# Rank terms of a channel attention on four row groups of the array, behind the value weights

## The reference

```
def _channel_attention(qm, km, vm, scale):
    qh, kh, vh = (heads of qm, km, vm as b, h, d, n)
    scores = jnp.einsum('bhdn,bhen->bhde', qh, kh) * scale
    attn = jax.nn.softmax(scores, axis=-1)
    out = jnp.einsum('bhde,bhen->bhdn', attn, vh)
...
att_global = _channel_attention(q * wqg + bqg, k * wkg + bkg, v * wvg + bvg, scale)
att_local = _channel_attention(q * wql + bql, k * wkl + bkl, v * wvl + bvl, scale)
xattn = 2.0 * (att_global + att_local) * wp + bp
x = x + tanh(g_xattn[0]) * xattn(_layernorm(x), ctx, ctx)
x = x + tanh(g_ffn[0]) * ffn(_layernorm(x))   # two linear layers, int8-like quantised, gelu
```

## Time and profile before

| | us |
|---|---|
| median of 3 runs | 369.76 (368.94 to 369.95) |
| the profiled execution, its own time | 368.73 |
| its span, first to last instruction | 366.9 |
| TensorE busy | 349.0 (95%) |
| VectorE busy | 330.2 (90%) |
| ScalarE busy | 285.2 (78%) |
| GpSimd busy | 119.8 (33%) |
| mean granted TensorE clock | 0.984 |

### The profile page before, as it was taken

One profiled execution on the slowest core, in us unless ns is written; L12 is line 12 of the kernel. 1 busy time (PEld: TensorE's weight loads), 2 busy tenths in 40 slices (PEclk: granted clock), 3 DMA queues, 4 the chain that ended last, 5 costly groups with the idle time before them and its releaser, 6 DMA issues.

```text
span 366.9 us, 6644 instructions
## 1 busy us (share of the span) xinstructions
PE 349.0 (95%) x2406; PEld 245.9 (67%) x2418; DVE 330.2 (90%) x630; ACT 285.2 (78%) x493; POOL 119.8 (33%) x178
## 2 busy tenths in 40 slices
PE   6979989999999888999999999999999999999995
PEld 4667767887886775554545455454548888888884
DVE  3698999999999978999999988987769999999996
ACT  1465879889886965879859988789799999999520
POOL 2644578778689790069000000421000000000000
PEclk9869999999999999999999999999999999999999
DMA  7999978565311463767748760000191999995225
GB/s 222 378 404 403 401 278 280 196 228 216 117 37 80 145 203 128 290 268 312 290 200 341 319 260 0 1 2 0 51 409 56 383 395 424 424 422 233 102 116 229
DMA packets 22963, 84.78 MB, mean 231 GB/s; under 512 B 2129, under 2 KB 11857, under 8 KB 14482
## 3 DMA queue, kind: packets, MB, share of 16 engines
q1 hardware_dynamic: 22272, 83.89, 59.2%
q10 hardware_dynamic: 658, 0.46, 0.4%
HBM read 54.99 MB, written 29.36 MB: 230 GB/s over the span
## 4 chain that ended last, share of the span: by engine, by line
PE 60%; DVE 19%; ACT 10%; issue 5%; DMA 3%; POOL 2%; SPq 1%; DVEq 0%; ACTq 0%; POOLq 0%
PE PS L1460 19%; PE PS L1415 17%; PE PS L1257 7%; DVE hmax L1042 7%; PE PS L1318 6%; ACT ring L703 5%; DMA X<-in_x 3%; PE PS L1299 3%; DVE hmax L832 2%; ACT ring L616 2%; PE PS L1266 2%; PE PS L1312 2%; DVE ring L1019 2%; PE PS L1289 1%; PE PS L1278 1%
## 5 line engine op out<-in xcount | busy, mean ns | idle before, releaser
L683 ACT ACTIVATE ring<-PS,bias,sc 128x512 f32<-128x512 f32 x128 | 97.1, 783 | 21.6 <-PE PS L1415 6.6
L1415 PE MATMUL PS<-mid,w1q 128*128 128x512 bf16 x500 | 110.7, 379 | 1.9 <-DVE mid L996 1.2
L1415 PEld LDWEIGHTS PS<-mid,w1q 128*128 128x128 bf16 x512 | 49.7, 98 | 59.9 <-DVE mid L996 0.7
L1042 DVE TENSOR_REDUCE hmax<-ring 128x1 f32<-128x2048 f32 x30 | 67.4, 2278 | 5.6 <-ACT ring L683 5.6
L703 ACT ACTIVATE ring<-ring,sc 128x2048 int16<-128x2048 f32 x29 | 55.6, 1987 | 0.0
L1460 PE MATMUL PS<-w2q,ring 128*128 128x256 f16 x336 | 39.0, 273 | 0.0
L1257 PE MATMUL PS<-ring 128*128 128x129 f32 x256 | 33.8, 296 | 2.0 <-DVE ring L741 1.5
L1460 PEld LDWEIGHTS PS<-w2q,ring 128*128 128x128 f16 x336 | 32.9, 98 | 4.0
L1257 PEld LDWEIGHTS PS<-ring 128*128 128x128 f32 x256 | 33.0, 212 | 3.1 <-issue 3.1
L1170 DVE SCALAR_TENSOR_TENSOR X<-PS,sc,X 128x512 f32<-128x512 f32 x48 | 35.0, 739 | 0.0
L1318 PEld LDWEIGHTS PS<-w2q,ring 128*128 128x128 f32 x256 | 29.2, 192 | 6.7 <-issue 6.7
(11 more groups left out here) (147 smaller groups left out, 586.8 us busy)
## 6 DMA issues: line engine op xcount, KB each, us to landing
spilled_hidden<-ring SPq DMA_DIRECT2D x20, 1024.0 KB, 3.9
ring<-spilled_hidden SPq DMA_DIRECT2D x20, 1024.0 KB, 9.1
ring<-in_ctxT SPq DMA_DIRECT2D x8, 1024.0 KB, 5.4
ring<-in_ctx SPq DMA_DIRECT2D x8, 896.0 KB, 8.4
X<-in_x SPq DMA_DIRECT2D x7, 1024.0 KB, 9.5
out<-X SPq DMA_DIRECT2D x7, 1024.0 KB, 9.6
ring<-in_w1T SPq DMA_DIRECT2D x4, 1024.0 KB, 13.4
ring<-in_w2T SPq DMA_DIRECT2D x8, 512.0 KB, 3.4
```

The costliest lines, as they stand in the source:

```text
L683: nc.scalar.activation(ring[:, s * CH + c, (h % CH) * N:(h % CH + 1) * N], PS[:, hidden_bank(s, h), :], ACT.Gelu, scale=SC1, bias=bias1[:, ...
L1042: V.tensor_reduce(hmax[:, bass.ds(CH * g + c, 1)], ring[:, s * CH + c, :], AX.X, ALU.max, apply_absolute_value=True).then_inc(hm_done, 1)
L1415: mm = nc.tensor.matmul(PS[:, hidden_bank(s, h), :], w1v[:, k, h * P:(h + 1) * P], xqT[:, s, k, :], start=(k == 0), stop=(k == NH - 1))
```

## The change

The rank terms become four products, one for each attention and each pair of heads, on the row groups 0 to 31, 32 to 63, 64 to 95 and 96 to 127, with 256 columns each, in banks 2, 3, 4 and 5 (the first half of each bank). `L_sb`, `Rh`, `rowc` and `psK` so have 128 partitions; `Rh`, `rowc` and `psK` have 256 columns. `sel` is wider and the key sums are two products of 256 columns. Since banks 2 and 3 are those of psT, the rank terms of batch b + 1 now wait for `m_done`, the value weights of batch b, which read psT. On VectorE the value weights go ahead of the constant row in passes 0 to 6. In pass 7 the warming products in bank 2 wait for the scores. The host lays out `blocks` and `turned` for the new places, `ones` moves to another buffer, and 64 more columns of `small` are used.

The diff, cut to its core (the layouts on the host and the widths of buffers are left out):

```
-        sel = cut(64)
+        sel = cut(P + 32)
...
-        Rh = mid[:, 0:512]
-        rowc = mid[:, 512:1024]
+        ones = w2f[:, 0:P]
+        Rh = mid[:, 0:2 * P]
+        rowc = mid[:, 512:512 + 2 * P]
...
-        psR = PS[:, 4:6, :].rearrange("p a (h e) -> p (a h) e", e=P)
-        psA = PS[0:64, 4, 0:P]
-        psK = PS[0:64, 5, :]
+        psR = PS[:, 2:6, 0:2 * P].rearrange("p q (h e) -> p q h e", e=P)
+        psA = PS[:, 4, 0:P]
+        psK = PS[:, 5, 0:2 * P]
...
-                nc.gpsimd.tensor_tensor(Rh[0:64, :], Rh[0:64, :], rowc[0:64, :], ALU.mult).then_inc(rh_done, 1)
+                nc.gpsimd.tensor_tensor(Rh, Rh, rowc, ALU.mult).then_inc(rh_done, 1)
...
-                nc.scalar.activation(L_sb[0:64, :], psA, ACT.Copy).then_inc(L_done, 1)
+                nc.scalar.activation(L_sb, psA, ACT.Copy).then_inc(L_done, 1)
...
                 elif b >= 0:
+                    value_weights(b)
                     constant_row(b)
                     if b == B - 2:
                         w1_scale()
-                    value_weights(b)
...
-                nc.tensor.matmul(psK, sel, ksum.rearrange("p h e -> p (h e)"), start=True, stop=True).then_inc(sk_done, 1)
+                for a in range(2):
+                    mm = nc.tensor.matmul(psK, sel[:, 32 - 32 * a:32 - 32 * a + P],
+                                          ksum[:, 2 * a:2 * a + 2].rearrange("p h e -> p (h e)"),
+                                          start=(a == 0), stop=(a == 1))
+                mm.then_inc(sk_done, 1)
...
                 pe.wait_ge(L_done, b + 1)
                 pe.wait_ge(rh_done, b + 1)
-                for g in range(2):
-                    mm = nc.tensor.matmul(PS[:, 4 + g, :], L_sb[32 * g:32 * g + 32, :], Rh[32 * g:32 * g + 32, :],
-                                          start=True, stop=True)
+                if b == 0:
+                    pe.wait_ge(scaled, 2 * NH)
+                else:
+                    pe.wait_ge(m_done, 4 * b)
+                for q in range(4):
+                    rows = slice(32 * q, 32 * q + 32)
+                    mm = nc.tensor.matmul(PS[:, 2 + q, 0:2 * P], L_sb[rows, :], Rh[rows, :], start=True, stop=True)
                 mm.then_inc(r_done, 1)
...
                     pe.wait_ge(tn_done, 2 * b)
+                    pe.wait_ge(s_done, 8 * B)
                     keep_warm(4, 2)
```

More of the change, by code:

```diff
@@ L64, in gated_xattn_ffn @@
         ident = sb("ident", [P, P], F32)
-        small = sb("small", [P, 528], F32)
+        small = sb("small", [P, 592], F32)
         taken = [0]
@@ L69, in part @@
             taken[0] += n
-            assert taken[0] <= 528
+            assert taken[0] <= 592
             return small[:, taken[0] - n:taken[0]]
@@ L74, in gated_xattn_ffn @@
         colv = part(9 * NH + KH)
-        acol = part(65)
+        acol = part(P + 1)
         st = part(NT * 6).rearrange("p (i e) -> p i e", e=6)
@@ L111, in gated_xattn_ffn @@
         row_vectors = sq_sb[0:1, 0:3, :].rearrange("p i d -> p (i d)")
-        ones = cut(P)
         w_stage = flat[:, 2 * CH * CW:]
@@ L433, in _ @@
             for g in range(2):
-                nc.gpsimd.memset(sel[:, 32 * g + NH:32 * g + 2 * NH], 1.0).then_inc(consts, 1)
+                nc.gpsimd.memset(sel[:, 64 * g + 34:64 * g + 36], 1.0).then_inc(consts, 1)
             for h in range(NH):
@@ L551, in _ @@
             act.dma_start(acol[:, :], turned).then_inc(blocks_in, 16)
-            act.dma_start(rowc[0:64, :], blocks).then_inc(blocks_in, 16)
+            act.dma_start(rowc, blocks).then_inc(blocks_in, 16)
             act.wait_ge(gates_in, 16)
@@ L586, in key_copy @@
                 act.wait_ge(r_done, b)
-                nc.scalar.activation(Rh[0:64, :], psK, ACT.Identity, scale=1.0, bias=acol[0:64, 64:65]).then_inc(kc_done, 1)
+                nc.scalar.activation(Rh, psK, ACT.Identity, scale=1.0, bias=acol[:, P:P + 1]).then_inc(kc_done, 1)
             def left_rows(b):
@@ L771, in columns @@
                 wq = colv[:, 0:8 * NH].rearrange("p (g c a h) -> p g c a h", g=2, c=4, a=2)[:, :, 0]
-                V.tensor_tensor(acol[:, 0:64].rearrange("p (g r a h) -> p g r a h", g=2, a=2, h=2)[:, :, 0],
+                V.tensor_tensor(acol[:, 0:P].rearrange("p (g a r h) -> p g r a h", g=2, a=2, h=2)[:, :, 0],
                                 sums_q, wq, ALU.mult).then_inc(a_done, 1)
@@ L789, in key_rows @@
                 wait(dve, r_done, b)
-                V.scalar_tensor_tensor(Rh[0:64, :], psK, acol[0:64, 64:65], rowc[0:64, :], ALU.add,
+                V.scalar_tensor_tensor(Rh, psK, acol[:, P:P + 1], rowc, ALU.add,
                                        ALU.mult).then_inc(rh_done, 1)
@@ L797, in scores @@
                 for j in range(2 * NH):
-                    V.tensor_tensor_reduce(S_sb[:, j, :], S_sb[:, j, :], psR[:, j, :], -SCALE, 3.0e38, ALU.add, ALU.min,
+                    V.tensor_tensor_reduce(S_sb[:, j, :], S_sb[:, j, :], psR[:, j // 2, j % 2, :], -SCALE, 3.0e38, ALU.add, ALU.min,
                                            nb[:, j:j + 1]).then_inc(s_done, 1)
@@ L1265, in key_sums @@
                 pe.wait_ge(ks_step, 3 * b + 3)
-                nc.tensor.matmul(psK, sel, ksum.rearrange("p h e -> p (h e)"), start=True, stop=True).then_inc(sk_done, 1)
+                for a in range(2):
[3 more added lines that the diff above has]
+                mm.then_inc(sk_done, 1)
             def turn_columns(b):
                 pe.wait_ge(a_done, b + 1)
-                nc.tensor.transpose(psA, acol[:, 0:64], ident[:, :]).then_inc(aT_done, 1)
+                nc.tensor.transpose(psA, acol[:, 0:P], ident[:, :]).then_inc(aT_done, 1)
             def rank_terms(b):
@@ L1536, in blocks @@
     def blocks():
-        m = np.zeros((2, 32, D), np.float32)
+        m = np.zeros((2, 2, 32, 2 * P), np.float32)
         for g, c in enumerate("gl"):
-            for r, n in enumerate(("bk", "wk", "bk")):
-                for h in range(NH):
-                    m[g, NH * r + h, h * P:(h + 1) * P] = vec(n + c)[h * P:(h + 1) * P]
-        return m.reshape(64, D)
+            for a in range(2):
+                for r, n in enumerate(("bk", "wk", "bk")):
+                    for h in range(2):
+                        m[g, a, 2 * r + h, h * P:(h + 1) * P] = vec(n + c)[(2 * a + h) * P:(2 * a + h + 1) * P]
+        return m.reshape(P, 2 * P)
     def turned():
-        m = np.zeros((P, 65), np.float32)
+        m = np.zeros((P, P + 1), np.float32)
         for g, c in enumerate("gl"):
-            for r in (1, 2):
-                m[:, 32 * g + NH * r:32 * g + NH * r + NH] = col(vec("bq" + c))
-            m[32 * g:32 * g + NH, 64] = 1.0
-            m[32 * g + 2 * NH:32 * g + 3 * NH, 64] = N
+            for a in range(2):
+                for r in (1, 2):
+                    m[:, 64 * g + 32 * a + 2 * r:64 * g + 32 * a + 2 * r + 2] = col(vec("bq" + c))[:, 2 * a:2 * a + 2]
+                m[64 * g + 32 * a:64 * g + 32 * a + 2, P] = 1.0
+                m[64 * g + 32 * a + 4:64 * g + 32 * a + 6, P] = N
         return m
```

## The result

| | before | after |
|---|---|---|
| median, us | 369.35 (367.3 to 369.95) | 373.49 (373.4 to 375.54) |
| profiled execution, us (its span) | 368.73 (366.9) | 373.54 (371.7) |
| attention passes 2 to 5, each, us | 13.45 | 14.35 |

The changed kernel is slower: the ratio of the times, from the comparison of the runs, is 1.0145, interval 1.012 to 1.0169. The time of 373.49 is just within the range (373.4 to 377.2) and 1.6 under the forecast of 375.1.

What follows compares the result with a forecast made beforehand. TensorE was taken to bound the loop, without slack in passes 2 to 5. 0.98 + 3.92 + 0.45, less up to 0.1, gave +5.3 us: 374.0 profiled, 375.1 as median with 1.03 added; range 373.4 to 377.2.

Steps and rivals of the forecast that it cites:

- The place and the mechanism: Corner between constant sums and value product: value weights go first, delaying constant row and first rows, with TensorE idle 1.2 us.
- The size of a pass: Passes 2 to 5: each gets 0.98 us longer, bounds 0.96 to 1.04, as the first rows wait for the constant row.
- The rank terms: TensorE, ahead of the first rows: four products take 0.43 us instead of 0.86, inside a wait of 0.63.
- Rival B: Rank terms hold TensorE's array longer than their 0.63 us cover: 376.5 us, or 381.6 one after the other; chance 0.13.
- That the shorter rank terms gain nothing: TensorE, rank terms: the 0.43 us saved is worth 0, because the first rows wait for the constant row anyway.
- rival C: Value weights done before the constant sums end, so TensorE gains 0.43 in passes 1 to 6: 367.2 us; chance 0.04.
- Scores, key rows, key sums at no cost: VectorE scores 0.2 us later but covered; shorter key rows worth 0; key sums 1.07 to 1.3 us, taken up by idle time.
- Pass 0: Later constant row hidden by pass 1's wait for GpSimd: 0, with up to 0.1 us gained from the shorter key row.
- Pass 1: VectorE is late there and the first rows wait for the constant row; the same exchange costs 0.98 us.
- rival E: A granted clock under 1.00 between 40 and 140 us; chance 0.07, its forms together.
- the dear form: The form of rival E with clock falls behind the holes of the passes; chance 0.07 together with the single form.
- Pass 6: Value product begins at 118.61 instead of 118.17, and this goes through to the loop's end: +0.45 us.

Runs made afterwards that it cites:

- e1: Kernel before with only the VectorE order changed, value weights ahead of the constant row; rank terms as before: 375.6 us, ratio 1.0175.
- e2: Changed kernel with the old VectorE order, constant row then value weights; rank terms still wait for the value weights: 388.42 us, ratio 1.0516.
- e4: Changed kernel with VectorE's largest square cut, one tile ahead of the value weights and three behind the scores: 367.97 us, ratio 0.9982.
- e10: e4 with the four value products of output tile 0 moved ahead of the first-row products on TensorE: 368.0 us, ratio 0.9992.
- e8: Kernel before with value weights first and the largest square cut, three of its four tiles behind the scores: 369.78 us, ratio 1.004.
- e6: Changed kernel with 9 warming products in pass 1, behind the waits for the two sides of the rank terms: 373.9 us, ratio 1.0128.
- e5: Changed kernel run once more, unedited: 374.34 us, ratio 1.0147 to the kernel before.
- e3: Changed kernel with 20 warming products in pass 1, ahead of all waits of the rank terms: 375.96 us, ratio 1.019.
- e7: e2 with warming products ahead of the rank terms from pass 0 on, 7 each and 12 in pass 1: 377.06 us, ratio 1.0218.

## Why the prediction was right, point by point

**The place and the mechanism.** That the chain of a pass goes from the largest square over the value weights and the constant row to the first rows was the core, and it holds: after's rows show both waits, and e1 shows that the order alone gives the whole loss.

**The size of a pass** was put at 0.98 (0.96 to 1.04) and is 0.90, under the lower bound. From the start of L804 the first rows start 3.96 later (88.91 to 92.87), against 3.04 before, which is 0.92; the sum had reached 4.00 at its lower end. Value weights start 2.19 behind L804, the overlap that was the lower end, the constant row 3.22, and the first rows 0.05 and not 0.07 behind its end. From the first rows to the chain's next Gram product it takes 4.91 (92.87 to 97.78), 0.02 less than before. Four passes so gave 3.60 and not 3.92.

**The rank terms** were put at 0.43 within a cover of 0.63. Both were off: e2 measures 0.51 for them, and the cover is 0.51 too (92.36 to 92.87), since the rank terms start 0.14 behind the last value weight, a delay that I hadn't charged. Rival B, that they outlast it, didn't come about: e1, with no such dependence, has the same pass within 0.01. But the margin was nil and not 0.20. The old shape took 0.86 and would by this have outlasted the cover; with the wait for the value weights it wasn't tried. The Trainium skill (TensorE: Matmul & The Clock Gate, Part 3, Measured speedup vs the span model) has four row groups 3.07 times as fast as one after the other, from which I had estimated 0.56; against 4 x 0.43 = 1.72 the measured 0.51 is 3.4 times, between that and the full 4 that I took.

**That the shorter rank terms gain nothing** where they stand was argued from the wait of the first rows for the constant row, 0.07 in the earlier trace rows. e4 and e10 bear it out twice over: even when VectorE makes room, the first rows wait for the constant row, or the time is lost at two more changes of shape; and the corner is as long with the old shape in e8. So the 0.43 a pass of rival C doesn't come in e4, though the value weights there end with the constant sums.

**Scores, key rows, key sums at no cost.** The scores waited 0.32 for the rank terms, and the four output tiles wait for the value product behind them, as said. GpSimd's key row takes 732 ns instead of 1265 and shows nowhere in passes 2 to 5. The key sums got shorter, not longer: 0.86 to the next start instead of 1.01. A wait of 0.20 for ScalarE takes all of it back: from the turn of the weights to the constant sums pass 4 takes 2.22 (86.83 to 89.05), against 2.21 (84.44 to 86.65).

**Pass 0** was put at 0, and at most 0.1 of gain. Its Gram product, before (first row) and after (second):

```profile
21.72 6.62 PE L1257 MATMUL PS<-ring 128*128 128x129 f32 x32 [1.54 <-DVE ring L741]
...
21.05 5.45 PE L1257 MATMUL PS<-ring 128*128 128x129 f32 x32 [1.35 <-DVE ring L741]
```

From the end of its Gram product to the largest square of pass 1 it takes 17.93 before (28.34 to 46.27) and 17.74 after (26.50 to 44.24): -0.19. TensorE lost half a microsecond in pass 0, where the rank terms waited 0.92 for the value weights (9.73 before and 10.27 after, from one Gram product's end to the next one's start), and the turn of the weights in pass 1, which waits for GpSimd, took it up, as the step said: 2.07 to the key sums before, 1.29 after.

**Pass 1** was put at 0.98. Before, in pass 1:

```profile
46.27 2.27 DVE L804 TENSOR_REDUCE small<-ring 128x4 f32<-128x2048 f32 x1
47.82 1.13 PE L1278 MATMUL PS<-mid,ring 32*128 32x512 f32 x4 [0.80 <-POOL mid L463]
53.96 3.74 PE L1257 MATMUL PS<-ring 128*128 128x129 f32 x32
```

and after, beside the rows of the result:

```profile
44.24 2.28 DVE L804 TENSOR_REDUCE small<-ring 128x4 f32<-128x2048 f32 x1
```

From its largest square to the next Gram product it takes 7.69 before (46.27 to 53.96) and 10.31 after (44.24 to 54.55): 2.62. Of this, 1.6 is the fall of the clock behind a hole of 2.68, as e6 shows, where without the fall it is 8.70, so +1.01. This is rival E in its single form, which had 0.07 with the dear form and a price of 3; it came true at 1.6, and with it the sign of being wrong that I had given for E, a granted clock under 1.00 between 40 and 140 us. The step that failed is the one on the hole: I took it as 1.2 everywhere, and didn't work out that in pass 1 TensorE is ahead of VectorE and would now wait there for all of it. The rows before held it: with the value weights in the constant row's place, from 48.46, the last of them would end at about 49.6, and the constant sums were done at 47.02, 0.80 ahead of the rank terms. That is 2.6 and not 1.2.

**Pass 6** was put at 0.45, and at 0.3 in the lower bound, for which no row was given. From the Gram product that begins pass 6 to the value product it comes to 0.54 (112.13 to 122.91, against 107.93 to 118.17). It goes through to the end, where 4.8 is left.

**What the sum hides.** The ledger of the two profiled executions: pass 0 -0.19, pass 1 +2.62, passes 2 to 5 +3.60, pass 6 +0.54, together 6.6. The execution of after reached the end of the Gram product of pass 0 at 26.50, that of before at 28.34, 1.84 earlier: 4.7 is left, and the spans differ by 4.8. The changed kernel itself reached that point at 26.43 in e5, and e6 and e3, which differ from it only behind that point, at 28.50 and 28.42. So this lead comes and goes with the execution and can't be booked to the change. Both profiles of the changed kernel were early ones and have the fall in pass 1; whether late executions have it too, without warming, isn't shown. The execution of e5 with a mean clock of 1.000 has none: its 374.83 stands 4.9 to 5.0 above the executions of the kernel before with 0.998 that ran beside it (369.79 to 369.96), and the ledger without the fall comes to 5.0. None of these has a profile; the agreement speaks for the other terms of the ledger.

**The dear form of E.** A hole of 1.2 us in each pass of 14.4 left the clock at 2.4 GHz, as I argued from the earlier trace rows; holes of 1.96 in e2 brought it down to 1.2 GHz in three of the passes 2 to 5, and one of 1.97 didn't. The row that I leaned on, a stretch in which TensorE was busy for 6.47 of 9.00 us, said little of a single hole: the order of e2, with holes only 0.7 us longer, comes out at 388. The Trainium skill (TensorE: Matmul & The Clock Gate, HAM oscillation — how this bites in real kernels) describes a loop that falls to the lower clock in each pass because it waits in each; e2's rows agree in three of the passes 2 to 5; the changed kernel's passes 2 to 6 don't show it.

## What to carry to other kernels

Before shortening an instruction, look at what the one behind it waits for: if another wait ends at the same moment, the shortening is worth nothing, and whatever delays that other wait costs in full. Exchanging two instructions on a full engine moves two consumers, and the one to price is the consumer that stands first in its own queue. Work out each new hole on TensorE pass by pass, also for the odd passes at the start, because a hole can cost the clock on top of its length.

## What the runs showed of the hardware

- Holes of 0.66 (e1) and 1.27 us (after), one in a pass, left the granted clock at 1.00; behind one of 1.96 us (e2) and one of 2.68 (after, pass 1) it fell to the level of 1.2 GHz, at a price of 1.6 us each time. One pass of e2 kept 2.4 GHz behind a hole of 1.97, and in pass 1 of e1 the clock fell behind holes of 0.80 and 1.28 with the rank terms between them, so the length of one hole alone doesn't decide.
- Added work that nobody reads made a kernel 11 us faster (e2 to e7).
- Four products of 256 columns on four row groups, 32 rows each, take 0.51 us to the next start; two of 512 columns on two row groups took 0.86.
- Two steps with one more change each between products of 32 and of 128 rows were longer by 0.30 us together (e10).
- GpSimd's multiply took 732 ns for 128x256 (L463, after), 1265 for 64x512 (L463, before) and 1090 for 128x512 (L455, before, with another input).
